# Selective scan in a fused Perceiver block: the seventh pass of each feature block as two scans of one state, with the product by C shared between VectorE and GpSimd

## The reference

```python
delta = jax.nn.softplus(jnp.einsum('blr,dr->bld', dt, dt_proj_w) + dt_proj_b)
A = -jnp.exp(A_log)
def step(hstate, t):
    delta_t, B_t, C_t, x_t = t
    dA = jnp.exp(delta_t[..., None] * A)
    dBx = (delta_t * x_t)[..., None] * B_t[:, None, :]
    hstate = dA * hstate + dBx
    y = jnp.einsum('bdn,bn->bd', hstate, C_t)
    return (hstate, y)
...
y = jnp.swapaxes(ys, 0, 1) + xin * D
return jnp.einsum('bld,ed->ble', y * jax.nn.silu(z), out_proj_w)
```

## Time and profile before

| What | Value |
|---|---|
| Runs | 2520.57, 2522.21, 2522.47 us; median 2522.21 |
| The profiled execution: its own time, its span | 2526.3 us, 2524.4 us |
| TensorE busy, matmul instructions | 2398.6 us, 14111 |
| VectorE busy | 1974.6 us |
| ScalarE busy | 1601.7 us |
| GpSimd busy | 669.9 us |
| Mean granted TensorE clock, share of full speed | 0.983 |

### The profile page before, as it was taken

The page is one execution under the profiler, slowest core; times in us unless marked ns, Lnnn a source line. Parts: engine busy times, 40 slices in busy tenths (PEclk is TensorE's granted clock), DMA queues, the critical chain, the costliest instruction groups (busy, mean ns, idle before and its releaser), DMA issues. The chain is left out here.

```text
span 2524.4 us, 39338 instructions
## 1 busy us (share of the span) xinstructions
PE 2398.6 (95%) x14111; PEld 1016.1 (40%) x14111; DVE 1974.6 (78%) x1972; ACT 1601.7 (63%) x1974; POOL 669.9 (27%) x461
## 2 busy tenths in 40 slices
PE   7999999999999799999999999999887778989998
PEld 3333333333333244444444444444332234444554
DVE  5777777777777788888988898988679993267996
ACT  5555555565555478777778877778384442237994
POOL 1455555555555400000000000000019990020001
PEclk9999999999999899999999999999989999999999
DMA  6245654455445593433334333433240005148994
GB/s 250 84 151 164 204 164 150 158 173 167 150 137 157 137 264 81 114 100 98 104 88 110 90 104 88 112 97 95 102 158 22 0 0 200 50 176 317 406 406 171
DMA packets 178206, 366.02 MB, mean 145 GB/s; under 512 B 19546, under 2 KB 90330, under 8 KB 174426
## 3 DMA queue, kind: packets, MB, share of 16 engines
q1 hardware_dynamic: 176610, 360.81, 44.8%
q0 software_dynamic: 1280, 4.20, 0.5%
q10 hardware_dynamic: 248, 0.15, 0.0%
HBM read 254.24 MB, written 106.68 MB: 143 GB/s over the span
## 5 line engine op out<-in xcount | busy, mean ns | idle before, releaser
L466 DVE TENSOR_REDUCE kv_mx<-kv_s 128x1024 f32 (+1 forms) x512 | 595.3, 1217 | 223.7 <-PE kv_s L502 223.7
L818 DVE TENSOR_TENSOR at_pl<-at_pf,at_ph 128x1024 f16<-128x1024 f32 x512 | 613.1, 1223 | 115.6 <-ACT at_ph L765 106.7
L771 ACT ACTIVATE at_pf<-at_st 128x1024 f32<-128x1024 f32 x512 | 497.3, 1025 | 190.3 <-PE at_st L939 137.5
L938 PE MATMUL at_st<-keep_big,at_k_cur 128*128 (+1 forms) x1024 | 390.6, 381 | 10.1 <-DMA keep_big<-q_dram 7.3
L939 PE MATMUL at_st<-keep_big,at_k_one 128*128 (+1 forms) x1024 | 389.1, 380 | 0.0
L765 ACT ACTIVATE at_ph<-at_pf 128x1024 f16<-128x1024 f32 x256 | 272.9, 1066 | 0.0
L1135 POOL MEMSET mamba_zero<- 128x2 f32 x1 | 0.1, 99 | 943.7 <-POOLq L60 943.7
L900 PE MATMUL at_acc<-at_ph,at_vs 128*128 128x512 f16 x1024 | 243.0, 380 | 3.4 <-DVE at_pl L818 3.3
L382 POOL TENSOR_TENSOR kv_ksl<-kv_kf,kv_ksh 128x512 f16<-128x512 f32 x128 | 147.9, 1156 | 247.4 <-ACT kv_ksh L410 247.4
L1049 PE MATMUL kv_kp<-first_ch,first_wkh 128*128 128x512 f16 x512 | 195.4, 382 | 6.1 <-DVEq L448 6.1
L407 ACT ACTIVATE kv_kf<-kv_kp,first_bks 128x512 f32<-128x512 f32 x128 | 87.3, 682 | 172.6 <-PE kv_kp L1049 172.6
(11 more groups left out here) (349 smaller groups left out, 3863.3 us busy)
## 6 DMA issues: line engine op xcount, KB each, us to landing
keep_big<-gate_up SPq DMA_DIRECT2D x17, 2048.0 KB, 13.0
at_vs<-vd SPq DMA_DIRECT2D x64, 512.0 KB, 3.9
at_k_cur<-kd SPq DMA_DIRECT2D x126, 256.0 KB, 3.8
vd<-kv_vs SPq DMA_DIRECT2D x15, 2048.0 KB, 7.7
kv_tf<-wpack SPq DMA_DIRECT2D x21, 1024.0 KB, 6.3
keep_big<-down SPq DMA_DIRECT2D x17, 1024.0 KB, 14.0
first_cf<-ctxT SPq DMA_DIRECT2D x16, 1024.0 KB, 12.2
ex_yg<-gate_up SPq DMA_DIRECT2D x8, 2048.0 KB, 13.6
```

Of the source, the lines that this page charges most:

```text
L466: nc.vector.reduce_max(mx[:, bass.ds(g * (NH * TT) + 2 * (m - TT), 2)], s1[:, m % 3, :, :], AX.X).then_inc(s1_max, 1)
L771: nc.scalar.activation(pf[:, s % FULL, :, :], st[:, s % HP % NST, :, :], ACT.Exp, scale=SCORE).then_inc(pf_ready, 1)
L818: nc.vector.tensor_tensor(pl[:, s % RING, :, :], pf[:, s % FULL, :, :], ph[:, s % RING, :, :], ALU.subtract).then_inc(pl_ready, 1)
L938: nc.tensor.matmul(st[:, w % NST, e, :], k_cur[:, tile], qh[:, q], start=True, stop=False)
```

## The change

Pass q = 6 (HALF) of each block is no longer one scan of both states with one product. VectorE now scans state 1 into hc, then scans state 0 in place in PSUM, waits for that scan (the new semaphore own_half) and multiplies state 0 by C into hc. State 1 is multiplied by C in place by GpSimd, which calls output(i) for this pass too, after b of pass i + 2. TensorE waits for both counters before it adds pass 6. GpSimd's b of pass i waits for own_half as well where pass i - 3 is a pass 6. pool_products(n) replaces pool_passes(n) where products on GpSimd are counted. The arithmetic is the same.

```diff
--- before.py
+++ after.py
@@ -1067,6 +1067,8 @@
 NOW_Z = 2
 
 POOL_OUT = (1, 4)
+
+HALF = 6
 
 
 def scan_rows(keep, first):
@@ -1327,7 +1329,7 @@
             m.sem(n) for n in ("own_dve", "next_in", "n_in", "var_ready", "sd_ready", "nws_ready"))
         h_ready, hT_ready, hh_ready, hl_ready = (m.sem(n) for n in ("h_ready", "hT_ready", "hh_ready", "hl_ready"))
         first_ready, zs_ready = m.sem("first_ready"), m.sem("zs_ready")
-        ss_ready, warm = m.sem("ss_ready"), m.sem("warm")
+        ss_ready, warm, own_half = m.sem("ss_ready"), m.sem("warm"), m.sem("own_half")
         da_ready, scanned, summed = (m.sem(n) for n in ("da_ready", "scanned", "summed"))
         dve_hc, pool_hc = m.sem("dve_hc"), m.sem("pool_hc")
         u_ready, b_ready, xk_ready = m.sem("u_ready"), m.sem("b_ready"), m.sem("xk_ready")
@@ -1341,6 +1343,9 @@
         def pool_passes(n):
             return n // PASSES * len(POOL_OUT) + sum(q in POOL_OUT for q in range(n % PASSES))
 
+        def pool_products(n):
+            return pool_passes(n) + n // PASSES + (n % PASSES > HALF)
+
         def wait_states(eng, i):
 
             if i % PASSES in POOL_OUT:
@@ -1350,9 +1355,11 @@
 
         def wait_outputs(eng, i):
             if i % PASSES in POOL_OUT:
-                eng.wait_ge(pool_hc, pool_passes(i + 1))
+                eng.wait_ge(pool_hc, pool_products(i + 1))
             else:
                 eng.wait_ge(dve_hc, i + 1 - pool_passes(i))
+                if i % PASSES == HALF:
+                    eng.wait_ge(pool_hc, pool_products(i + 1))
 
         @block.sync
         def _(sp):
@@ -1366,7 +1373,7 @@
             sp.wait_ge(b_ready, NP - 1)
             load_gates(sp, keep, wsplit, slice(0, DF // 2), next_in, (0,))
             sp.wait_ge(dve_hc, NP - pool_passes(NP))
-            sp.wait_ge(pool_hc, pool_passes(NP))
+            sp.wait_ge(pool_hc, pool_products(NP))
             load_gates(sp, keep, wsplit, slice(0, DF // 2), next_in, (1,))
             sp.wait_ge(next_in, 64)
 
@@ -1377,7 +1384,9 @@
                 pool.wait_ge(scanned, i + 1)
                 if i < PASSES:
                     pool.wait_ge(c_in[q], 16)
-                nc.gpsimd.tensor_tensor(hc[i % RC][:, :, :], hc[i % RC][:, :, :], cc[q], ALU.mult).then_inc(pool_hc, 1)
+                ns = slice(1, HN) if q == HALF else slice(0, HN)
+                nc.gpsimd.tensor_tensor(hc[i % RC][:, ns, :], hc[i % RC][:, ns, :], cc[q][:, ns, :],
+                                        ALU.mult).then_inc(pool_hc, 1)
 
             for i, (f, q) in enumerate(passes):
                 if q == 0 and f:
@@ -1386,15 +1395,17 @@
                     pool.wait_ge(u_ready, f)
                 if i >= RB:
                     pool.wait_ge(scanned, i - RB + 1)
+                    if (i - RB) % PASSES == HALF:
+                        pool.wait_ge(own_half, (i - RB) // PASSES + 1)
                 if i == 1:
                     pool.wait_ge(first_ready, 1)
                 if i:
                     nc.gpsimd.tensor_tensor(b[i % RB][:, :, :], u[:, :].unsqueeze(1).to_broadcast([P, HN, T]),
                                             bb[q], ALU.mult).then_inc(b_ready, 1)
-                if i >= RB - 1 and (i - RB + 1) % PASSES in POOL_OUT:
+                if i >= RB - 1 and (i - RB + 1) % PASSES in POOL_OUT + (HALF,):
                     output(i - RB + 1)
             for i in range(NP - RB + 1, NP):
-                if i % PASSES in POOL_OUT:
+                if i % PASSES in POOL_OUT + (HALF,):
                     output(i)
 
         @block.scalar
@@ -1452,10 +1463,20 @@
                 if i >= RC:
                     dve.wait_ge(summed, i - RC + 1)
                 out = hc[i % RC][:, :, :]
-                nc.vector.tensor_tensor_scan((out if q in POOL_OUT else h).rearrange("p n t -> p (n t)"), flat,
-                                             b[i % RB].rearrange("p n t -> p (n t)"), 0.0,
-                                             ALU.mult, ALU.add).then_inc(scanned, 1)
-                if q not in POOL_OUT:
+                if q == HALF:
+                    nc.vector.tensor_tensor_scan(out[:, 1, :], h[:, 1, :], b[i % RB][:, 1, :], 0.0, ALU.mult,
+                                                 ALU.add).then_inc(scanned, 1)
+                    nc.vector.tensor_tensor_scan(h[:, 0, :], h[:, 0, :], b[i % RB][:, 0, :], 0.0, ALU.mult,
+                                                 ALU.add).then_inc(own_half, 1)
+                    dve.wait_ge(own_half, f + 1)
+                    if f == 0:
+                        dve.wait_ge(c_in[q], 16)
+                    nc.vector.tensor_tensor(out[:, 0, :], h[:, 0, :], cc[q][:, 0, :], ALU.mult).then_inc(dve_hc, 1)
+                else:
+                    nc.vector.tensor_tensor_scan((out if q in POOL_OUT else h).rearrange("p n t -> p (n t)"), flat,
+                                                 b[i % RB].rearrange("p n t -> p (n t)"), 0.0,
+                                                 ALU.mult, ALU.add).then_inc(scanned, 1)
+                if q not in POOL_OUT + (HALF,):
                     dve.wait_ge(scanned, i + 1)
                     if f == 0:
                         dve.wait_ge(c_in[q], 16)
```

## The result

| | us |
|---|---|
| Kernel before, median of 6 runs (2520.57 to 2525.25) | 2522.57 |
| Changed kernel, median of 6 runs (2531.64 to 2536.21) | 2533.36 |
| Ratio, with its 95% interval | 1.004 (1.0029 to 1.005) |
| Predicted | 2529.6 (2521.5 to 2533.5) |

The change made the kernel 0.4% slower, 10.8 us between the medians. In the profiled execution the span is 2534.3 us against 2524.4. The scan stage, from the start of the first scan to that of the last gate, took 2097.47 - 1879.77 = 217.70 us against 2090.62 - 1881.08 = 209.54, so 8.16 of the 9.9 us lie in it. The other 1.7 us lie outside the stage, where the edits change nothing.

What follows compares the result with a forecast made beforehand. VectorE was taken to bound the scan stage, GpSimd close behind. First gate -0.11, six blocks +0.48, last block -0.48 and five slow blocks +7.50 gave +7.4 us on 2522.2: 2529.6 us, range 2521.5 to 2533.5.

Steps and rivals of the forecast that it cites:

- VectorE saves 0.48 a block: VectorE, pass 6: scan and product of 3.46 us replaced by half scans and half product of 2.98; bounds 0.24 to 0.54.
- GpSimd's half is 1.27 us long: GpSimd queue: one added 512-wide product, step 1.24 us, lifts its loop from 24.58 to 25.82 us, above the earlier 25.74.
- The sums of q=6 and q=7 become late: TensorE: eight matmuls wait for GpSimd's half, run 1958.78 to 1962.48; the gate is 0.37 us late even at full clock.
- The clock falls over that burst: TensorE, sums of q=6 and q=7: after 3.61 us idle the clock drops in some blocks, costing 1.69 us each.
- A slow block takes 27.32 us: Loop through TensorE's sums and the gate: 25.63 us plus 1.69 for a clock fall, 1.50 more per block hit.
- Five of the seven are slow: Blocks 0 to 6: share of clock falls taken from the kernel before; five slow blocks add 7.50 us.
- rival 1: TensorE's clock falls over the q=6 and q=7 sums in all seven blocks: +10.6 us, 2532.8; chance 0.16.
- The sum: Over seven gates with a block behind them: -0.11 us at full clock, +7.50 for slow blocks, total +7.4 us.
- Rival 2: TensorE's clock stays up over the new burst, or falls in at most three blocks: 2522.1 to 2526.6 us; chance 0.32.
- Rival 3: GpSimd's half product costs nearly a whole one, loop up to 26.89 us: +8 us, 2530; chance 0.04.
- rival 5: VectorE's half scans cost more than thought: its loop 25.50, sum unchanged but 0.24 at the end; no separate chance.
- rival 4: VectorE's saving arrives whole in all eight blocks: -3.8 us, 2518.4; needs a GpSimd loop of 25.26; chance 0.03.

Runs made afterwards that it cites:

- run 1: Changed kernel plus zero matmuls filling TensorE's gaps before the sums of q=4 and q=6 in every block: 2525.84 us, ratio 1.001.
- run 2: Changed kernel plus zero matmuls filling TensorE's gaps before the sums of q=4 and q=6, except in the last block: 2522.12 us, ratio 0.9998.
- run 5: Kernel before plus seven spare GpSimd products of the half's size, at the same queue place, on data nothing waits for: 2522.64 us, ratio 1.000.
- run 3: Control: kernel before plus the zero matmuls ahead of the sums of q=4 and q=6, except in the last block: 2523.82 us, ratio 1.000.
- third execution: Changed kernel, unaltered, profiled a third time: all seven blocks slow, scan stage 220.55 us.
- run 7: Kernel before with only pass 6's scan split in two, one whole product on VectorE, nothing added on GpSimd: 2524.27 us, ratio 1.0001.
- run 4: Changed kernel with VectorE's gate of the previous block moved from behind the product of pass 0 to behind the scan of pass 1: 2527.18 us, ratio 1.0013.
- run 6: Changed kernel with GpSimd's half product of pass 6 moved ahead of u and the next block's b of pass 0: 2521.88 us, ratio 0.9992.

## Why the prediction was right, and where it was off

- **VectorE saves 0.48 a block.** Measured 3.46 - 2.98 = 0.48; the halves' steps are 1.13 and 1.24, the half product's 0.61. Right to 0.01.
- **GpSimd's half is 1.27 us long, its loop becomes 25.82, and it takes over as the bound.** 1.27 is right, and so is the bound: in the quick loops GpSimd never waits, and its queue takes 25.76 to 25.78 us (runs 1, 2 and 5). The way over the sums and the gate is nearly as long: in run 1 the scan of q=1 ends 0.15 us before GpSimd's product of q=1 starts, where the pick-up takes 0.08 when GpSimd waits for it. The loop was 0.05 us too dear, a step of 1.24 for 1.23 and the rest in small differences that I added up.
- **The sums of q=6 and q=7 become late, run as one burst of eight, and the gate waits.** Right: 0.41 to 0.44 us at the full clock (0.37 predicted) from the second gate on, shown by runs 1 and 2. TensorE picks the half up 0.14 us after its end (1957.79 to 1957.93), where 0.05 was taken.
- **The clock falls over that burst.** Right, and shown as the cause: with the clock kept up the loss is gone (run 2), with the clock kept up where no one waits nothing is gained (run 3). Which blocks it hits I had wrong. In front of the first slow burst of the profiled execution the burst of q=4 and q=5 itself had run slow and TensorE then stood 2.00 us (block 2), where I had taken a gap of 1.92 as too short for a second fall. In all slow blocks of this execution both bursts are slow. (The third execution has the expected kind too, in its first two blocks: a quick burst of 3.70, a gap of 3.70 and 3.69 us, and then the slow one of 5.37.)
- **A slow block takes 27.32 us.** Measured 27.38 to 27.46; the burst takes 1.70 us more (5.37 against 3.67; 1.69 predicted), and the later pick-up accounts for the rest.
- **Five of the seven are slow.** Five, five and seven in three executions. That it was five in two of them is partly luck: I took the share from how often the clock fell before, as if each block drew anew, and the rows show otherwise: once a block was slow, every later one was. The sum with seven, +10.6, was rival 1's, and the measured 10.8 is nearest to it, but two of the three profiled executions had five. By the Trainium skill, "TensorE: Matmul & The Clock Gate", section "Why this matters for your kernels", gaps between bursts of matmuls cost the clock. Taken strictly, that rule gave rival 1's number. The third execution agrees with it, the two others don't, and in them bursts ran slow behind gaps of 2.00 us, shorter than those that the section warns of.
- **The sum.** +7.4 was worked out, and the stage of the profiled execution has +8.16: the first gate is 0.26 later instead of 0.11 earlier (in the first block VectorE waited 0.51 us for a transfer and 0.17 at the gate), the quick loop gives 0.03, the loops of the five slow blocks 8.3 instead of 7.9, the last -0.47. The other 2.6 us of the 10.8 between the medians are more slow blocks or the rest of the program; no run decides it. So 2533.36 lies inside the range, but only 0.1 us under its end.
- **A row that I read wrongly.** The 0.73 us in front of the sum of q=7 is how long TensorE stood idle until VectorE's product ended, and not the time from the product to the sum, which is 0.06. The working goes by the start at 1959.31, so nothing changes.
- **The last block gives 0.48 back.** 24.56 against 25.03: 0.47.
- **Rivals.** Rival 2 (no fall) did not happen by itself; with the clock kept up (run 2) its stage came out: 209.24 us, 0.3 under the kernel before, where 0.1 was worked out. Rival 3 (a dear half) falls by the 1.27 us that the half took and by run 5, rival 5 (a dear split) by run 7, and rival 4 (the whole saving) did not come, as GpSimd's loop would have had to be 25.26 and is 25.76.

## What to carry to other kernels

When a bound engine hands work to one with slack, ask where in the second engine's queue the work goes and who waits for its result: with the same half product the stage took 8.2 us more behind the next b and 1.5 us less in front of u, one profile each (for the whole kernel: 10.8 us more, and no difference that the runs can tell). An engine that is idle a fifth of the time can still be the one that sets the pace, if its work is bunched up right in front of a wait. And where a burst of matmuls behind a gap gets onto the path, price it at both levels of TensorE's clock.

## What was not expected of the hardware

- Slow blocks stay slow in the changed kernel. In three executions (5, 5 and 7 slow blocks of 7) no quick block followed a slow one, and the slow loops agree to 0.02 us, 27.38 to 27.40, but for the first of two executions, 27.46. In the kernel before, at a loop of 25.74, slow and quick bursts of q=4 came mixed, and with the gate later (run 4) a quick burst of q=6 (3.67 us, block 1) followed a slow one (5.37, block 0). Why they stay slow is not shown.
- A gap of 2.00 us behind a burst that ran slow was followed by a second slow burst, in five blocks out of five; a gap of 2.18 us behind one that took 5.23 us was not (block 1).
- An operation on GpSimd can hide the wait of the next one for its own engine's result: with the half product between b and u, GpSimd's loop was 25.64 us (run 6), where the same instructions took 25.77 in the other order (run 1), in both without a wait for another engine.
